# A state-space and expert block on one core: joins of state rows move from VectorE to ScalarE, with one 1 MB accumulating transfer per state

## What is computed

```python
def step(s, inp):
    d_t, B_t, C_t, u_t = inp
    dA = jnp.exp(d_t[..., None] * A)
    dBu = d_t[..., None] * B_t[:, None, :] * u_t[..., None]
    s = s * dA + dBu
    y = jnp.einsum('bds,bs->bd', s, C_t)
    return (s, y)
...
return ys.swapaxes(0, 1) + u * D
...
y = y * jax.nn.silu(z)
out = jnp.einsum('bld,ed->ble', y, out_proj_w)
```

## Time and profile before

| | us |
|---|---|
| median of 3 runs (lowest to highest) | 2739.45 (2736.83 to 2739.89) |
| profiled execution, span | 2736.3 |
| VectorE busy | 2398.1 (88%) |
| TensorE busy | 2351.9 (86%) |
| GpSimd busy | 2256.4 (82%) |
| ScalarE busy | 1945.8 (71%) |

### The profile page before, as it was taken

The page is one execution under the profiler, slowest core; times in us unless marked ns, Lnnn a source line. Parts: engine busy times, 40 slices in busy tenths (PEclk is TensorE's granted clock), DMA queues, the critical chain, the costliest instruction groups (busy, mean ns, idle before and its releaser), DMA issues.

```text
span 2736.3 us, 51736 instructions
## 1 busy us (share of the span) xinstructions
PE 2351.9 (86%) x16084; PEld 1889.2 (69%) x16084; DVE 2398.1 (88%) x3815; ACT 1945.8 (71%) x3713; POOL 2256.4 (82%) x2222
## 2 busy tenths in 40 slices
PE   3456998989899898989989898998989898898989
PEld 1334777867677686767768676776867677686867
DVE  4879999898998989899998989989898999988853
ACT  4786867778686777867677786767878676785631
POOL 1777898989889798988989889897989979897932
PEclk7667999999999999999999999999999999999999
DMA  2564665646466564656657565665756566565721
GB/s 80 164 143 108 146 148 137 162 115 154 121 145 156 137 161 113 151 130 148 147 132 168 120 145 121 155 156 122 163 114 153 130 159 147 117 156 134 155 70 55
DMA packets 131520, 372.07 MB, mean 136 GB/s; under 512 B 19720, under 2 KB 22408, under 8 KB 130992
## 3 DMA queue, kind: packets, MB, share of 16 engines
q0 software_dynamic: 50688, 184.57, 36.4%
q1 hardware_dynamic: 80560, 184.20, 20.4%
HBM read 166.29 MB, written 17.87 MB: 67 GB/s over the span
## 4 chain that ended last, share of the span: by engine, by line
POOL 30%; issue 22%; PE 20%; DVE 13%; ACT 7%; DMA 2%; POOLq 1%; DVEq 0%; ACTq 0%; SPq 0%
POOL db_sb L713 16%; PE bank_ps L1480 7%; DVE states L1196 5%; PE moe_ps L1498 5%; POOL act L756 4%; PE rows_ps L1416 4%; POOL y_sb L725 3%; POOL y_sb L734 2%; ACT da_ps L957 2%; PE bank_ps L1376 2%; ACT c_rows L930 1%; POOL du_sb L700 1%; DMA w_sb<-w_dram 1%; DVE act L1296 1%; DVE bank_ps L1143 1%
## 5 line engine op out<-in xcount | busy, mean ns | idle before, releaser
L713 POOL TENSOR_TENSOR db_sb<-du_sb,b_sb 128x512 f32<-128x512 f32 x1024 | 1473.6, 1655 | 32.8 <-DVE states L1196 32.2
L957 ACT ACTIVATE da_ps<-delta,a_sb 128x512 f32<-128x512 f32 x1024 | 696.6, 689 | 170.4 <-DVE states L1196 168.2
L1416 PE MATMUL rows_ps<-ident,states 128*128 128x128 f32 x4096 | 611.4, 287 | 120.9 <-DVE states L1196 85.2
L1480 PE MATMUL bank_ps<-h2T_high,ein_w_high 128*128 128x256 f16 x2304 | 633.9, 275 | 83.8 <-DVE act L1302 50.0
L1196 DVE TENSOR_TENSOR_SCAN states<-da_ps,carry,db_sb 128x512 f32<-128x512 f32 x512 | 644.9, 1273 | 19.0 <-ACT da_ps L957 17.6
L1416 PEld LDWEIGHTS rows_ps<-ident,states 128*128 128x128 f32 x4096 | 503.3, 148 | 210.6 <-DVE states L1196 98.0
L1196 DVE TENSOR_TENSOR_SCAN states<-da_ps,db_sb 128x512 f32<-128x512 f32 x512 | 613.9, 1213 | 34.5 <-ACT da_ps L957 26.3
L1480 PE MATMUL bank_ps<-h2T_low,ein_w_high 128*128 128x256 f16 x2304 | 634.0, 275 | 0.0
L1480 PE MATMUL bank_ps<-h2T_high,ein_w_low 128*128 128x256 f16 x2304 | 633.6, 275 | 0.0
L1498 PE MATMUL moe_ps<-eout_sb,act 128*128 128x256 f32 x2304 | 583.3, 387 | 41.5 <-POOL act L756 40.7
L756 POOL TENSOR_TENSOR act<-act,w_sb 128x256 f32<-128x256 f32 x512 | 472.9, 1115 | 164.0 <-DVE act L1302 141.7
(11 more groups left out here) (170 smaller groups left out, 2671.2 us busy)
## 6 DMA issues: line engine op xcount, KB each, us to landing
y_sb<-c_rows POOLq DMA_DIRECT2D x352, 512.0 KB, 5.5
b_sb<-b_dram SPq DMA_DIRECT2D x128, 512.0 KB, 4.8
w_sb<-w_dram SPq DMA_DIRECT2D x256, 256.0 KB, 3.5
th_p<-x_dram SPq DMA_DIRECT2D x16, 512.0 KB, 5.2
r_dram<-conv SPq DMA_DIRECT2D x16, 512.0 KB, 4.3
x<-r_dram SPq DMA_DIRECT2D x16, 512.0 KB, 3.5
out_dram<-x SPq DMA_DIRECT2D x32, 256.0 KB, 3.6
mod_p<-mod_dram SPq DMA_DIRECT2D x7, 384.0 KB, 4.5
```

Source lines behind the costliest of these rows:

```text
L713: pool.tensor_tensor(db_sb[:, n % NDB, :], du_sb[:, slots[t][0][0], b, :], b_sb[:, k % NBPAIR, s % BPAIR, :], ALU.mult).then_inc(sem["scal ...
L957: ac.activation(da_ps[n % NDA][:, :], delta[:, slots[t][0][0], b, :], ACT.Exp, scale=a_sb[:, b, s:s + 1]).then_inc(sem["exp_done"], 1)
L1416: last = pe.transpose(rows_ps[j % 2][:, b * P:b * P + P], states[:, step % 2 * NB + b, j * P:j * P + P], ident[:, :])
L1480: last = pe.matmul(bank(key)[:, a * HALF:a * HALF + HALF], ein_w16[w][:, k, e // 2, at:at + HID], h2T[h][:, k, q * HALF:q * HALF + HALF], ...
```

## The change

Joins on VectorE go. JOINED becomes empty: the rows of states 0 to 14 are all scaled by ScalarE into c_rows, and the last state's are joined to y on VectorE as before. c_rows becomes two buffers (NCR) of all four pieces, 8 KB per partition, and a state is added to y by one accumulating transfer of 1 MB: 15 per chunk in place of 22. There is one semaphore for the adds; each waits for the one before it. The four pieces' scalings of a state must be done before its add, and `y_join` of every piece waits for the whole add of state 14.

```diff
-NDA, NDB, NCR = 2, 5, 3
-CPAIR = 2
-JOINED = (1, 5, 9, 13)
+NDA, NDB, NCR = 2, 5, 2
+JOINED = ()
...
-            if j % CPAIR == CPAIR - 1 and s + 1 not in JOINED and s < NS - 1:
-                out.append((at + 0.892, ("c_add", t, s, j // CPAIR)))
+            if j == NJ - 1 and s + 1 not in JOINED and s < NS - 1:
+                out.append((at + 0.892, ("c_add", t, s)))
...
-        c_rows = sb("c_rows", [P, NCR, CPAIR, DI])
+        c_rows = sb("c_rows", [P, NCR, NJ, DI])
...
-            def piece(step, j):
+            def piece(step):
 
                 k, s = divmod(step, NS)
-                return NJ // CPAIR * ((NS - 1 - len(JOINED)) * k + s - sum(q <= s for q in JOINED)) + j // CPAIR
+                return (NS - 1 - len(JOINED)) * k + s - sum(q <= s for q in JOINED)
 
             def c_adds(n):
 
-                return sem[f"c_added{n % (NJ // CPAIR)}"], 16 * (n // (NJ // CPAIR) + 1)
+                return sem["c_added"], 16 * (n + 1)
...
-                    def c_add(t, s, pair):
+                    def c_add(t, s):
 
                         step = NS * nS(t) + s
-                        n = piece(step, CPAIR * pair)
-                        pool.wait_ge(*c_scales(step, CPAIR * pair + CPAIR - 1))
-
-                        if step:
-                            pool.wait_ge(*c_adds(n - NJ // CPAIR))
-                        if s == 0 and t > 0 and slots[t - 1][1] is not None:
+                        n = piece(step)
+                        pool.wait_ge(*c_scales(step, NJ - 1))
+
+                        if n:
+                            pool.wait_ge(*c_adds(n - 1))
+                        if s == (1 if 1 in JOINED else 0) and t > 0 and slots[t - 1][1] is not None:
                             pool.wait_ge(*bank_read(("skip_t", t - 1, NB - 1)))
-                        pool.dma_start(y_sb[:, slots[t][0][0], CPAIR * pair:CPAIR * pair + CPAIR, :], c_rows[:, n % NCR, :, :],
-                                       accum_op=ALU.add).then_inc(c_adds(n)[0], 16)
+                        pool.dma_start(y_sb[:, slots[t][0][0], :, :], c_rows[:, n % NCR, :, :], accum_op=ALU.add).then_inc(c_adds(n)[0], 16)
...
                     def c_scale(t, s, j):
 
                         step = NS * nS(t) + s
-                        n = piece(step, j)
+                        n = piece(step)
                         ac.wait_ge(sem["rows_full"], NJ * step + j + 1)
+                        if s == 0 and j == 0:
+                            ac.wait_ge(*bank_read(("xd_t", t - 1)))
                         if n >= NCR:
                             ac.wait_ge(*c_adds(n - NCR))
-                        ac.activation(c_rows[:, n % NCR, j % CPAIR, :], rows_ps[j % 2][:, :], ACT.Copy,
+                        ac.activation(c_rows[:, n % NCR, j, :], rows_ps[j % 2][:, :], ACT.Copy,
                                       scale=xd_sb[:, slots[t][0][0], j, s:s + 1]).then_inc(sem["c_scaled"], 1)
...
                     def xd_t_evac(t):
                         key = ("xd_t", t)
+                        if nS(t):
+                            v.wait_ge(*c_scales(NS * nS(t) - 2, NJ - 1))
...
+                        if not JOINED and j == 0:
+                            v.wait_ge(*bank_read(("xd_t", t - 1)))
                         v.wait_ge(sem["rows_full"], NJ * step + j + 1)
-                        v.wait_ge(*c_adds(piece(step - 1, j)))
+                        v.wait_ge(*c_adds(piece(step - 1)))
```

```diff
+SHIFT = {"b_load": 0.786, "b_store": -4.694, "c_add": 1.332, "c_scale": 0.773, "carry": 2.848, "delta": 0.935, "dt_bias": 0.427,
...
+PLACE = {"b_load_0": 0.049, "b_load_1": 15.075, "b_load_2": 8.921, "b_load_3": 8.338, "b_load_4": 7.439, "b_load_5": 5.417,
+         "b_load_6": 5.818, "b_load_7": 5.004, "b_store": 13.849, "c_add_0": -0.865, "c_add_1": 1.962, "c_add_10": -0.288,
+         "c_add_11": -0.37, "c_add_12": -1.018, "c_add_13": -0.709, "c_add_14": 3.548, "c_add_2": 1.146, "c_add_3": 0.08, "c_add_4": -0.237,
+         "c_add_5": 1.292, "c_add_6": 0.477, "c_add_7": 1.32, "c_add_8": 1.31, "c_add_9": -0.83, "c_scale_0": -0.483, "c_scale_1": -2.092,
+         "c_scale_2": 0.114, "c_scale_3": -0.613, "carry_0": -3.163, "carry_1": -0.908, "carry_10": -2.958, "carry_11": -1.155,
```

More of the change, by code:

```diff
@@ L145 @@
 SLOT = 70.5212
[L146 to L160, removed]
@@ new lines @@
+NEAR_LAST = {"b_load": -3.266, "c_add": -1.134, "c_scale": -0.658, "carry": -7.886, "e_act": 1.495, "e_mul": 1.393, "e_tanh": -0.312,
+             "e_weigh": -0.82, "exp": -1.407, "expert_in": -2.082, "expert_out": -0.692, "h2_high": 1.62, "h2_low": 2.53,
+             "h2_scale": -0.467, "h2_t": -1.305, "logit": -3.18, "logit_exp": 1.409, "mod_m_load": 0.52, "op": -1.474, "op_gate": -1.604,
+             "out_add": -0.571, "out_gate": -0.997, "out_store": -8.071, "r_load": 9.505, "router": -0.031, "rows": -1.72, "scaled": -1.053,
+             "scan": -1.668, "w_evac": 2.074, "w_load": -4.312, "w_store": 5.923, "w_t": -3.677, "x1": -1.442, "x1_norm": -0.21,
+             "x1_rstd": 0.595, "x1_stat": -1.349, "y_evac": -2.578, "y_gate": -2.027, "y_join": -0.906, "y_t": -1.624, "z": -2.636,
+             "z_gate": -3.378, "z_tanh": -2.584}
@@ L255, in place @@
+START = {"a_made": 15.78, "constants": -35.018, "ct_silu": -31.555, "ct_tanh": -17.126, "first_loads": 4.008, "fold": -5.963,
+         "in_high": -5.961, "in_low": -6.236, "mod0": -7.819, "mod0_gate": -22.44, "mod0_rows": -25.493, "mod_rows": 0.989,
+         "mod_store": 0.833, "mods": -23.966, "norm_lift": -15.926, "out_scale": 10.746}
 def place(what):
-    return "_".join(str(n) for n in (what[0], *(what[3:] if what[0] in ("exp", "scaled", "scan", "rows", "c_scale", "c_join", "y_join", "c_add") else what[2:])))
+    return "_".join(str(n) for n in (what[0], *(what[3:] if what[0] in ("exp", "scaled", "scan", "rows", "c_scale", "c_join", "y_join") else what[2:])))
@@ L265, in start_steps, with early_loads @@
     return out
-def schedule(slots, load_mod_p, load_mod_m):
-    out = [(SLOT * t - 0.95, t, 0, ("mod_m_load", t)) for t in load_mod_m]
-    out += [(SLOT * t - LEAD_P + 0.5, t, 0, ("mod_p_load", t)) for t in load_mod_p]
-    out += [(at - LEAD_P0 + START.get(what[0], 0.0), -1, 0, what) for at, what in start_steps()]
-    out += [(SLOT - 2, 0, 0, ("eout_load",)), (SLOT + 20, 0, 0, ("eout_fold",))]
+def early_loads():
+    out = [(SLOT - 2, ("eout_load",)), (SLOT + 20, ("eout_fold",))]
     for n in range(NPAIR):
@@ L275, in schedule @@
         at = SLOT + 2 + 6.5 * n
-        out += [(at - 10, 0, 0, ("ein_load", n)), (at, 0, 0, ("ein_high", n)), (at + 0.6, 0, 0, ("ein_low", n))]
-    latest = {}
-    for t, (s, p, m) in enumerate(slots):
-        steps = []
+        out += [(at - 10, ("ein_load", n)), (at, ("ein_high", n)), (at + 0.6, ("ein_low", n))]
+    return out
+def schedule(slots, load_mod_p, load_mod_m):
+    last = len(slots) - 1
+    ends = {0: FIRST, 1: SECOND, last - 1: NEAR_LAST, last: LAST}
+    listed = [(at - LEAD_P0, START.get(what[0], 0.0), 0.0, 0.0, what) for at, what in start_steps()]
+    for t, (s, p, m) in enumerate(slots):
+        mine = []
+        if t in load_mod_m:
+            mine.append((-0.95, ("mod_m_load", t)))
+        if t in load_mod_p:
+            mine.append((0.5 - LEAD_P, ("mod_p_load", t)))
+        if t == 0:
+            mine += early_loads()
@@ L280, in schedule @@
         if s is not None:
-            steps += scan_steps(t)
+            mine += scan_steps(t)
         if p is not None:
-            steps += [(at - (LEAD_P0 if t == 0 else LEAD_P), what) for at, what in prepare_steps(t)]
+            mine += [(at - (LEAD_P0 if t == 0 else LEAD_P), what) for at, what in prepare_steps(t)]
         if m is not None:
-            steps += [(at - LEAD_M if t == 0 else at, what) for at, what in mix_steps(t)]
-        ends = FIRST if t == 0 else LAST if t == len(slots) - 1 else {}
@@ L288, in schedule @@
-        for n, (at, what) in enumerate(steps):
-            at = round(at + SLOT * t + SHIFT.get(what[0], 0.0) + PLACE.get(place(what), 0.0) + ends.get(what[0], 0.0), 5)
-            latest[what[0]] = max(at, latest.get(what[0], at))
-            out.append((latest[what[0]], t, n, what))
-    order = [what for _, _, _, what in sorted(out, key=lambda x: (x[0], x[1], x[2]))]
+            mine += [(at - LEAD_M if t == 0 else at, what) for at, what in mix_steps(t)]
+        listed += [(at + SLOT * t, SHIFT.get(what[0], 0.0), PLACE.get(place(what), 0.0), ends.get(t, {}).get(what[0], 0.0), what) for at, what in mine]
@@ L294, in schedule @@
+    latest, keyed = {}, []
+    for n, (at, shift, own, end, what) in enumerate(listed):
+        at = at + shift + own + end
+        latest[what[0]] = max(at, latest.get(what[0], at))
+        keyed.append((latest[what[0]], n, what))
+    order = [what for _, _, what in sorted(keyed)]
     at = {what: n for n, what in enumerate(order)}
@@ L1234, in c_join @@
                         step = NS * nS(t) + s
```

(4 more changed lines are left out.)

63 lines of the change are left out of this document (39 added, 24 removed), and 141 rows, old and new, of the table PLACE.

## The result

The changed kernel takes 2713.9 us (median of 4 runs, 2710.0 to 2718.9) against 2739.3 before: a ratio (time after over time before) of 0.9911, 95% interval 0.9897 to 0.9925, 25 us faster. The profiled execution took 2713.55 us with a span of 2711.7, 24.6 us under the span before.

What follows compares the result with a forecast made beforehand. The prediction took VectorE, TensorE and GpSimd, within 5% of each other, and a chain of waits passing between engines as the bound. Per chunk -1.98 - 1.9 + 1.0 = -2.9 us, times 16 is -46: 2693 us, range 2620 to 2800.

Steps and rivals of the forecast that it cites:

- Joins and scalings: Per chunk VectorE loses 11.35 us of joins, 1.98 on the chain; ScalarE takes on 10.9 us of scalings, costing 0.
- Issues: GpSimd's transfers per chunk fall from 22 to 15 at 0.88 us each: 6.2 us saved, 1.9 on the chain.
- Rival B: On GpSimd each 1 MB issue takes twice as long: slower, 2760 us, chance 0.06.
- The 1 MB add: On the accumulating queue a 1 MB add lands in 8.3 us median, bounds 8.0 and 11.
- rival A: Chain of adds, each awaiting the previous landing, sets the pace: slower, 2805 us at a 9.6 us landing; chance 0.22.
- the room: Between a state's add and the next writing of its buffer: 4.0 planner units or 9.1 us, less for later adds.
- The sum of -3.9 us per chunk: Whole period: joins -1.98 and issues -1.9; also heaviest engine TensorE 143.1 plus 13 us, 156.1.
- VectorE's 9.4 us "beside other work": Rest of VectorE's 11.35 us of joins per chunk, beside other work or making room its successors can't use at once.
- rival D: VectorE was the bound, so most of its 11.35 us returns: under 2640 us, period under 153 us, chance 0.12.
- C: On VectorE and GpSimd, time saved turns into longer waits and nothing reaches the path: same, 2739 us, chance 0.10.
- The end of a chunk: Last joins on VectorE wait for state 14's whole add: 1.0 us per chunk, bounds 0 and 2.9.
- Order and ends: New order tables, bounded at the kernel's start and end: cost 0, with 20 us either way for the range.

Runs made afterwards that it cites:

- e1: Changed kernel with each add carrying two of a state's four row pieces, 512 KB instead of 1 MB: 2628.6 us.
- e10: Changed kernel with each add carrying three of a state's four row pieces, 768 KB instead of 1 MB: 2638.4 us.
- e9: Kernel before, each 512 KB add carrying only the first piece of its pair, 256 KB: 2738.3 us.
- e7: Changed kernel's work in the order worked out from the tables of the kernel before: 2931.6 us.
- e8: Kernel before's work in the order worked out from the tables of the changed kernel: 2836.4 us.
- e11: Changed kernel with the adds of states 3, 12 and 14 placed later in GpSimd's order: 2769.3 us.
- e6: Changed kernel with each 1 MB add issued as two 512 KB adds, each waiting only for its own half of the state before: 2726.2 us.
- e5: Changed kernel with every second state's add sent to a DRAM buffer, each add waiting for the one two before: 2664.8 us.

## Why the prediction came out as it did

The time lies on the side forecast and in the range; the gain is 25 us and not 46, the period 158.4 us (13 middle periods) where 156 to 158 was said. Step by step:

**Joins and scalings.** VectorE lost 7.6 us per chunk of the 11.35, ScalarE took on 7.0 instead of 10.9. Counts and durations stand (16 instructions of 739 and 689 ns); what the sum overlooked is that they overlap their neighbours:

```profile
L954 ACT ACTIVATE c_rows<-rows_ps,xd_sb 128x512 f32<-128x512 f32 x120 | 76.0, 689 | 13.3 <-PE rows_ps L1446 11.0 <-DMA y_sb<-c_rows 1.9
```

120 scalings of 689 ns are 82.7 us, and the engine was busy with them for 76.0, since busy time counts a stretch once where two records overlap. For VectorE the joins overlapped each other little (32 x 739 ns is 23.6 us against 22.7 in the earlier trace rows) and other instructions more: added up record by record over the nine periods, VectorE's instructions fell from 161.6 to 150.1 us per chunk, 11.5, as the sum has it, while the overlap among them fell from 14.7 to 10.8. That is the whole difference to 7.6. ScalarE stayed the least busy of the four engines of the earlier trace rows; that its added work cost nothing was not tried apart.

**Issues.** Right: 886 ns median, 34560 / 240 = 144 packets, so an 8 KB row is one packet; GpSimd 133.6 us per chunk, forecast 134.1. Rival B fell.

**The 1 MB add.** Landing 7.8 us, estimated 8.3 with a low bound of 8.0. The queue held 48.1% of the span, 5.43 us per transfer, where 2 x 2.83 was reckoned. Of the loads beside it the routing weights landed later, as said (5.1 us median, before 3.5), the B rows did not (4.5, before 4.8). By the formula of the Trainium skill (DMA: Bandwidth & Descriptors, Anatomy of one DMA) 1 MB would need an estimated 4.4 us, 1.2 more than 512 KB; the adds of this case needed 7.8, 2.3 more than in the earlier trace rows, so the trace, not the page, is to be used for accumulation. By the page's step rival A would have had next to no chance, and it is A's mechanism that ruled the second half of each chunk.

**Rival A, the step that failed.** The mechanism was described rightly and judged harmless at this landing. The mis-sized term is the room: 9.1 us between states, taken from the planner's units as a mean over the chunk. In the stretch where it decides states come 7.70 us apart (e1), so with 0.6 us from landing to the next issue the break-even is a landing of 7.1 us, not 9.3. Measured there 7.9: 0.8 us too much on each of five links, and some on the links before. Against A I had held that 512 KB adds made hardly anyone wait; 5.5 + 0.6 is 6.1 us, under 7.7, and says nothing of 1 MB.

**The gain ahead of it.** The sum of -3.9 us per chunk for joins and issues was too small for what the change gives, order included. Where the queue is slack (e10) a period is 153.7 us against 160.3, -6.6, and the time is 102 us under the kernel before, with a quarter of the adds' bytes left out (in the kernel before, e9 found no gain in leaving out half). What of this belongs to VectorE's 9.4 us "beside other work", as rival D has it, and what to the order worked out for the joins' absence, stays open, since e7 and e8 show neither without the other; D's sign, a period under 153 us, did not show. C (nothing reaches the path) fell as a forecast, but its mechanism shows in part. ScalarE's wait for VectorE's scans fell, and VectorE's for ScalarE's part of the experts grew (before, then after, whole run):

```profile
ACT da_ps L957 <- DVE states L1196: 168.2, 183, 3.8
DVE act L1296 <- ACT act L1023: 145.7, 147, 2.7
```

```profile
DVE act L1326 <- ACT act L1047: 209.4, 201, 4.0
...
ACT da_ps L981 <- DVE states L1222: 52.3, 95, 2.6
```

Two errors of opposite sign, some 55 us more gained than forecast and some 75 given back to the queue, met in a forecast 20 us off; that it came so near is luck.

**The end of a chunk.** Taken at 1.0 us. VectorE waited there for the last add 7.0 us in the whole run, 0.4 per chunk, but those behind the joins wait longer than before: TensorE's weight loads 40.6 us (before 2.5), GpSimd's gating 24.9 (3.5). In e1, where no join waits for an add, these two are 33.0 and 28.1, so most of it does not come from the landing. What it costs was not tried apart; e11 shows that a later last add is paid for, together with a later add of state 3.

**Order and ends.** The start cost 5.5 us and the tail gave 4.1, inside the 20 allowed. The bound was drawn too narrowly all the same: e7 and e8 put the price of a wrong order at 96 to 218 us.

## What to carry to other kernels

A chain in which each transfer waits for the landing of the last is a resource with a rate of its own: one link per landing plus the step to the next issue. Compare that with the pace at which its work arrives in the densest stretch, not with the mean over a period, and change one size (three quarters of the bytes, half of them) to see whether the cost sets in at a certain size or goes with every byte. An engine's idle time ahead of such a transfer isn't free time: work put in front of it delays the chain.

## What the runs showed of the hardware

Accumulating transfers on GpSimd's queue to 128 partitions landed after some 2.5 us plus about 1.3 us per 256 KB, an estimate from the four medians below. The same line of the list of issues (KB each, median us to landing) in e9, e1, e10 and after:

```profile
y_sb<-c_rows POOLq DMA_DIRECT2D x352, 256.0 KB, 3.8
```

```profile
y_sb<-c_rows POOLq DMA_DIRECT2D x240, 512.0 KB, 4.9
```

```profile
y_sb<-c_rows POOLq DMA_DIRECT2D x240, 768.0 KB, 6.5
```

```profile
y_sb<-c_rows POOLq DMA_DIRECT2D x240, 1024.0 KB, 7.8
```

Two of them in flight land later. In the kernel before, by the times of issue and landing, the 28 adds that were in flight beside no other landed after 4.6 us (median), the 84 that were for 3 us or more beside a neighbour after 6.1. In e6 the halves land after 6.6 us, where the same size took 4.9 in e1, one at a time; 478 of e6's 480 are in flight for 3 us or more beside a neighbour:

```profile
y_sb<-c_rows POOLq DMA_DIRECT2D x480, 512.0 KB, 6.6
```

With a second target (e5) an add was in flight together with the next in 99 of 239 places only, for 0.9 us at the median there. The adds into SBUF landed after 8.1 us, and those into DRAM were hardly slower:

```profile
y_sb<-c_rows POOLq DMA_DIRECT2D x120, 1024.0 KB, 8.1
elsewhere<-c_rows POOLq DMA_DIRECT2D x120, 1024.0 KB, 8.3
```
